# Bf16 term splitting through PSUM, a bf16 spike product and per-head exponentials in a four-layer kernel

## The reference

```
# layers 0 and 3: projections
q = (h @ Wq) * 8 ** -0.5;  k = h @ Wk;  v = h @ Wv
# layer 2, feed-forward of the spiking block; lif_scan is a leaky integrate-and-fire scan over tokens
s1 = lif_scan(x1 @ W1.T + b1)          # 0 or 1, 512 features
s2 = lif_scan(s1 @ W2.T + b2)          # 128 features
# layer 3, latent attention
p = softmax(gq @ gk.T + causal)        # 8 heads, 64 latents per query
```

## Time and profile before

| | us |
|---|---|
| median of 3 runs (lowest to highest) | 1788.99 (1785.4 to 1790.18) |
| profiled execution, its own time | 1789.75 |
| its span, first to last instruction | 1788.0 |
| DVE busy | 1332.3 (75%) |
| PE busy | 1250.5 (70%) |
| ACT busy | 879.0 (49%) |
| POOL busy | 248.0 (14%) |

### The profile page before, as it was taken

One profiled execution on the slowest core, in us unless ns is written; L12 is line 12 of the kernel. 1 busy time (PEld: TensorE's weight loads), 2 busy tenths in 40 slices (PEclk: granted clock), 3 DMA queues, 4 the chain that ended last, 5 costly groups with the idle time before them and its releaser, 6 DMA issues. The chain is left out here.

```text
span 1788.0 us, 29542 instructions
## 1 busy us (share of the span) xinstructions
PE 1250.5 (70%) x10539; PEld 612.1 (34%) x10540; DVE 1332.3 (75%) x3509; ACT 879.0 (49%) x1678; POOL 248.0 (14%) x274
## 2 busy tenths in 40 slices
PE   4799999999999997566973543040314789833776
PEld 2122222222222224346962431020113456622445
DVE  5899999999999953365448236959697779667773
ACT  4079999999999996221211113040002446612453
POOL 4000000000000000013310333030003231100223
PEclk9589999999999999667995676575655797965668
DMA  1101100001000000000004431000001402021000
GB/s 56 49 2 28 28 21 20 20 26 30 22 20 20 20 2 16 1 28 1 1 1 181 112 77 33 0 1 1 0 0 38 140 11 52 21 103 56 21 22 30
DMA packets 43229, 58.57 MB, mean 33 GB/s; under 512 B 11993, under 2 KB 33564, under 8 KB 42684
## 3 DMA queue, kind: packets, MB, share of 16 engines
q1 hardware_dynamic: 37851, 49.95, 9.4%
q0 software_dynamic: 3968, 6.01, 1.3%
q10 hardware_dynamic: 1264, 0.72, 0.2%
HBM read 29.81 MB, written 13.63 MB: 24 GB/s over the span
## 5 line engine op out<-in xcount | busy, mean ns | idle before, releaser
L724 ACT ACTIVATE l0att_probs<-l0att_ps_sv 128x512 f32<-128x512 f32 x1024 | 555.9, 595 | 84.4 <-PE l0att_ps_sv L694 72.6
L761 DVE TENSOR_REDUCE l0att_half_negmax<-l0att_ps_m 128x1 f32<-128x1024 f32 x480 | 547.2, 1215 | 6.3 <-PE l0att_ps_m L633 6.3
L663 PE MATMUL l0att_ps_sv<-l0att_probs,l_V_aug 128*32 128x256 f32 x4096 | 331.2, 392 | 5.3 <-ACT l0att_pv_sb L715 5.3
L694 PE MATMUL l0att_ps_sv<-l_Q,l_K 51*128 51x512 bf16 x1024 | 201.0, 389 | 2.5 <-ACT l0att_probs L724 0.2
L633 PE MATMUL l0att_ps_m<-l_K,l_Q 48*128 48x512 bf16 x960 | 186.1, 385 | 11.1 <-DVE l0att_half_negmax L761 7.1
L663 PEld LDWEIGHTS l0att_ps_sv<-l0att_probs,l_V_aug 128*32 128x32 f32 x4096 | 83.3, 108 | 199.1 <-issue 104.7
L694 PEld LDWEIGHTS l0att_ps_sv<-l_Q,l_K 51*128 51x128 bf16 x1024 | 49.6, 93 | 216.7 <-ACT l0att_probs L724 204.1
L350 PE MATMUL ada_ps<-ident_sb,xn 128*128 128x128 f32 x112 | 31.3, 442 | 87.5 <-DVE xn L338 87.0
L413 POOL CAST l0att_nm<-l0att_negmax 128x16 bf16<-128x16 f32 x16 | 3.2, 198 | 514.1 <-DVE l0att_negmax L737 514.1
L2554 ACT ACTIVATE l3loc_probs<-l3loc_ps_s 128x320 f32<-128x320 f32 x128 | 48.9, 435 | 36.1 <-PE l3loc_ps_s L2533 35.5
L2030 PE MATMUL l2spk_ps<-l_X,l_spikes_l_w2T 128*128 128x512 f32 x32 | 16.5, 680 | 68.3 <-DVE l_X L2054 68.3
(11 more groups left out here) (598 smaller groups left out, 2355.9 us busy)
## 6 DMA issues: line engine op xcount, KB each, us to landing
l_Q<-l_qp SPq DMA_DIRECT2D x188, 32.0 KB
l_K<-l_kp SPq DMA_DIRECT2D x188, 32.0 KB
l1ffn_W<-in_l_expert_w_dram SPq DMA_DIRECT2D x1, 4096.0 KB
l3f_experts_l_w<-in_l_w_dram SPq DMA_DIRECT2D x2, 2048.0 KB
l_sorted_in<-l1ffn_zeros SPq DMA_DIRECT2D x1, 3072.0 KB
l1exp_rows<-l_sorted_in SPq DMA_DIRECT2D x6, 512.0 KB, 8.5
l_sorted_out<-l1exp_y SPq DMA_DIRECT2D x6, 512.0 KB
l_Q<-l_q_parts SPq DMA_DIRECT2D x18, 128.0 KB
```

The costliest lines, as they stand in the source:

```text
L663: mm = pe.matmul(ps_v[32 * c:32 * c + 32, cols], V_aug[:, kt, h, :], probs[:, kt % 2, c, cols], start=(kt == 0 and part == 0), stop=(kt == ...
L694: pe.matmul(ps_s[:, (n + i) % 3, :], K[at, h % HEAD_BUFS, c1(kt)], Q[at, h % HEAD_BUFS, c4(2 * pair + i)], start=True, stop=True).then_inc ...
L724: act.activation(probs[:, kt % 2, c, :], ps_s[:, n % 3, :], ACT.Exp).then_inc(expd, 1)
L761: dve.tensor_reduce(half_negmax[:, h % 2, t, half:half + 1], src, AX_X, ALU.max, negate=True).then_inc(m_read, 1)
```

## The change

Projections: after ScalarE has copied a chunk as its first bf16 term, TensorE subtracts that term in the same PSUM bank, by a bf16 matmul with the negative identity; VectorE copies the remainder as the second term, TensorE subtracts that too, and VectorE (even chunks) or ScalarE (odd) copies the third. k comes ahead of q. The factor of q is put into its weights. The float32 copy of q is made in layer 3 alone, which uses it. VectorE's and GpSimd's splitting is gone, and each term is stored when its four chunks are there.

Spikes: the first spikes are written as bf16; the weights are split into three bf16 terms during the scan; each chunk is multiplied by three terms. Every chunk's sum is released by itself and ScalarE and VectorE copy two each.

Latent: for four of the eight heads ScalarE takes the exponential straight from PSUM, with the maximum as bias, and sums it in the same instruction; the other four go as before.

Masks: DMAs of GpSimd's queue place them with all heads in buffers 0 and 1, in place of DMAs of SyncE and copies by VectorE; ScalarE copies buffer 0 to buffer 2 as before.

The core of the diff (new semaphores and changed signatures left out):

```diff
@@ stage_project_parts @@
+def stage_project_parts(nc, loads, w_name, g, name, V_aug, qp, kp, q=None, drams=(), stored=None, beside=None):
+    CHUNKS = 2 * NC4
...
+        def term(n, i):
+            return (kp, qp)[n // NC4][i][:, c4(n % NC4)]
+                for m, (parts, dram) in enumerate(zip((kp, qp), drams)):
+                    read = NC4 * (m + 1)
+                    sp.wait_ge(high_read, read)
+                    sp.dma_start(dram[0], parts[0][:]).then_inc(stored, 16)
+                    sp.wait_ge(middle_read, read)
+                    sp.dma_start(dram[1], parts[1][:]).then_inc(stored, 16)
+                    for done in low_read:
+                        sp.wait_ge(done, read // 2)
+                    sp.dma_start(dram[2], parts[2][:]).then_inc(stored, 16)
+                for s in range(CHUNKS + 4):
+                    if s < CHUNKS:
+                        if s == NC4:
+                            pe.wait_ge(scaled, 1)
+                        pe.matmul(ps[:, s, :], w[:, 1 - s // NC4, :], g.hT[:, c4(s % NC4)], start=True, stop=True,
+                                  skip_group_check=True).then_inc(full_done, 1)
+                    if 2 <= s < CHUNKS + 2:
+                        n = s - 2
+                        pe.wait_ge(high_read, n + 1)
+                        pe.matmul(ps[:, n, :], minus[:], term(n, 0), start=False, stop=True,
+                                  skip_group_check=True).then_inc(rest_done, 1)
+                    if s >= 4:
+                        n = s - 4
+                        pe.wait_ge(middle_read, n + 1)
+                        pe.matmul(ps[:, n, :], minus[:], term(n, 1), start=False, stop=True,
+                                  skip_group_check=True).then_inc(last_done, 1)
+                    if s >= CHUNKS:
+                        j = s - CHUNKS
+                        pe.wait_ge(low_read[j % 2], j // 2 + 1)
+                        for t in range(4 * j, 4 * j + 4):
+                            mm = pe.matmul(ps[:, j, c1(t % 4)], g.hT[:, c1(t)], w[:, 2, :], start=True, stop=True)
+                act.wait_ge(loads.done, loads.all)
+                act.activation(w[:, 0, :], w[:, 0, :], ACT.Identity, scale=L0_K ** -0.5).then_inc(scaled, 1)
+                for s in range(CHUNKS + 4):
+                    if s < CHUNKS:
+                        act.wait_ge(full_done, s + 1)
+                        if q is not None and s >= NC4:
+                            act.activation(q[:, c4(s - NC4)], ps[:, s, :], ACT.Identity)
+                        act.activation(term(s, 0), ps[:, s, :], ACT.Identity).then_inc(high_read, 1)
+                    n = s - 4
+                    if n >= 0 and n % 2 == 1:
+                        act.wait_ge(last_done, n + 1)
+                        act.activation(term(n, 2), ps[:, n, :], ACT.Identity).then_inc(low_read[1], 1)
+                    j = s - CHUNKS
+                    if j >= 0:
+                        act.wait_ge(v_done, j + 1)
+                        act.activation(V_aug[:, 4 * j:4 * j + 4, :, 0:L0_K],
+                                       ps[:, j, :].rearrange("p (t h k) -> p t h k", t=4, h=L0_H), ACT.Identity)
+                for s in range(CHUNKS + 2):
+                    if s < CHUNKS:
+                        dve.wait_ge(rest_done, s + 1)
+                        dve.tensor_copy(term(s, 1), ps[:, s, :]).then_inc(middle_read, 1)
+                    n = s - 2
+                    if n >= 0 and n % 2 == 0:
+                        dve.wait_ge(last_done, n + 1)
+                        dve.tensor_copy(term(n, 2), ps[:, n, :]).then_inc(low_read[0], 1)
+                if beside is not None:
+                    beside(pool)
@@ stage_l2_spikes @@
+        w2_terms = st.sb("w2_terms", [P, 3, 4, P], BF16)
+        hidden = X[:, 0:2, :].rearrange("p g s -> p (g s)").bitcast(BF16).rearrange("p (g s) -> p g s", g=4)
+                pe.matmul(ps_t[:, 0, :], g.ident[:], w2[:].rearrange("p f e -> p (f e)"), start=True, stop=True,
+                          skip_group_check=True).then_inc(term_left, 1)
+                for i in range(2):
+                    pe.wait_ge(term_read, i + 1)
+                    pe.matmul(ps_t[:, 0, :], minus[:], w2_terms[:, i].rearrange("p f e -> p (f e)"), start=False,
+                              stop=True, skip_group_check=True).then_inc(term_left, 1)
+                pe.wait_ge(term_read, 3)
-                        mm = pe.matmul(ps[:, j, :], w2[:, f, :], X[:, f, c4(j)], start=(f == 0), stop=(f == 3))
-                mm.then_inc(h2_done, 1)
+                        for i in range(3):
+                            mm = pe.matmul(ps[:, j, :], w2_terms[:, i, f, :], hidden[:, f, c4(j)],
+                                           start=(f == 0 and i == 0), stop=(f == 3 and i == 2), skip_group_check=True)
+                        if f == 3:
+                            mm.then_inc(h2_done, 1)
+                for i in range(3):
+                    act.wait_ge(term_left, i + 1)
+                    act.activation(w2_terms[:, i].rearrange("p f e -> p (f e)"), ps_t[:, 0, :],
+                                   ACT.Identity).then_inc(term_read, 1)
-                act.wait_ge(h2_done, 1)
-                for j in range(NC4):
+                for j in range(0, NC4, 2):
+                    act.wait_ge(h2_done, j + 1)
...
+                    dve.tensor_scalar(by_chunk(hidden[:, f, :], HIDDEN_LENGTH),
-                dve.wait_ge(h2_copied, NC4)
+                dve.wait_ge(bias_ready, 1)
+                for j in range(1, NC4, 2):
+                    dve.wait_ge(h2_done, j + 1)
+                    dve.tensor_scalar(tokens_of(in_steps, OUT_LENGTH, 0, j), by_chunk(ps[:, j, :], OUT_LENGTH), 0.5,
+                                      half_b[:], ALU.mult, ALU.add).then_inc(h2_by_vector, 1)
+                dve.wait_ge(h2_copied, NC4 // 2)
+                dve.wait_ge(h2_by_vector, NC4 // 2)
@@ layer2_spiking @@
+        for_spikes = Loads(nc, d, st, "spikes", "l2_w2T", "l2_b2", "minus16")
...
+def load_mask_rows(eng, d, Q, K, buf, placed):
...
+        eng.dma_start(operand[buf][0:MASK_ROWS],
+                      bcast(d[name].unsqueeze(1), MASK_ROWS, GROUP, S + WINDOW)).then_inc(placed, 16)
@@ stage_l3_latent @@
+    SUMMED = 4
-                        pe.wait_ge(sub_ready, t - 3)
+                        pe.wait_ge(expd, t - 3)
-                        act.activation(probs[:, t % PROBS], sc[:, t % 2], ACT.Exp).then_inc(expd, 1)
+                        if t >= 2:
+                            act.wait_ge(rden_ready, t - 1)
+                        for h in range(SUMMED):
+                            act.activation(probs[:, t % PROBS, h, :],
+                                           ps_a[:, t % 4, h * LATENTS:(h + 1) * LATENTS], ACT.Exp,
+                                           bias=neg_top[:, t % 2, h:h + 1], accum_out=den[:, t % 2, h:h + 1])
+                        act.activation(probs[:, t % PROBS, SUMMED:], sc[:, t % 2], ACT.Exp).then_inc(expd, 1)
...
-                        link(dve.tensor_reduce(top[:, b, :], s3, AX_X, ALU.max))
...
+                        dve.tensor_reduce(neg_top[:, b, :], s3, AX_X, ALU.max, negate=True).then_inc(top_ready, 1)
+                        dve.wait_ge(top_ready, t + 1)
+                        dve.tensor_tensor(sc[:, b], s3[:, SUMMED:, :],
+                                          bcast(neg_top[:, b, SUMMED:].unsqueeze(2), P, LAT_H - SUMMED, LATENTS),
+                                          ALU.add).then_inc(sub_ready, 1)
-                        link(dve.tensor_reduce(den[:, b, :], probs[:, pb], AX_X, ALU.add))
+                        link(dve.tensor_reduce(den[:, b, SUMMED:], probs[:, pb, SUMMED:], AX_X, ALU.add))
@@ stage_l3_local @@
-                            pe.wait_ge(mask_copied[grp % GROUP_BUFS], 2)
+                            if grp % GROUP_BUFS < 2:
+                                pe.wait_ge(mask_placed[grp % GROUP_BUFS], 16 * 2)
+                            else:
+                                pe.wait_ge(mask_copied, 2)
+                act.wait_ge(mask_placed[0], 16 * 2)
...
+                    act.activation(operand[2][0:MASK_ROWS], operand[0][0:MASK_ROWS], ACT.Identity)\
+                       .then_inc(mask_copied, 1)
@@ layer3_attention @@
+        for_parts = Loads(nc, d, st, "parts", "l3_wqkv", "minus16")
...
-        load_mask_rows(nc.sync, d, Q, K, mask_placed)
+        mask_placed = [st.sem(f"mask_placed{b}") for b in range(2)]
...
+            def load_masks(pool):
+                for b in range(2):
+                    load_mask_rows(pool, d, Q, K, b, mask_placed[b])
+            stage_project_parts(nc, for_parts, "l3_wqkv", g, "l3proj", V_aug, qp, kp, q, (k_parts, q_parts), stored,
+                                load_masks)
@@ lay_out @@
-        "ident16": bits16(np.eye(P)),
+        "ident16": bits16(np.eye(P)), "minus16": bits16(-np.eye(P)),
```

(51 more changed lines are left out.)

66 lines of the change are left out of this document (14 added, 52 removed).

## The result

The changed kernel takes 1765.88 us (median; 1763.52 to 1768.7, 4 runs) against 1789.08 us before: ratio 0.9873, 95% interval [0.9858, 0.9888]. Forecast were 1772 and a range of 1762 to 1783. The profiled execution has a span of 1766.3 us, 21.7 less than before.

A forecast was written before the change was run, and what follows sets the result against it. Stages follow one another behind barriers; VectorE's chain bounds the projections, a ring over all engines the latent loop. Terms -6.6 - 1.7 - 3.3 - 2.7 - 3.0 = -17.3 against 1789.75 gave 1772.5, so 1772; range 1762 to 1783.

The forecast's parts named there:

- Layer 2 product: Layer 2 spikes product: 48 bf16 matmuls replace 32 fp32 passes and one last copy replaces four, scan starts 6.6 us earlier.
- Layer 0 projection: Layer 0 q and k splitting leaves VectorE; TensorE becomes the bound, stage ends at 39.1 instead of 40.79, -1.7 us.
- a change from bf16 back to fp32 weights: Projections on TensorE: each switch of weights takes 0.31 instead of 0.215 us, 12 times 0.1, adding 1.2 us.
- switches free: Layer 0 projection's lower bound: the changes of weights on TensorE cost nothing, -2.9 us.
- Layer 3 projection: Layer 3: the same added 4.6 us on TensorE, next matmul at 1398.7 instead of 1402.03, -3.3 us.
- Head of the latent stage: Layer 3 latent stage's first eight passes run at the high clock after shorter idle time, 3.6 instead of 6.31 us, -2.7.
- Latent loop: Layer 3 loop: subtraction and sum fall from eight heads to four; last 11 tiles gain 0.27 us each, -3.0.
- Ring: Latent loop's round over all four engines, two tiles: falls from 6.28 to 5.74 us.
- Rival (a): ScalarE bounds the latent loop: at 0.67 us per head a tile takes 3.7 us, whole kernel 1783; chance 0.12.
- Rival (b): Layer 3 mask transfers crowd the DMA engines, local stage 5.5 us late, whole kernel 1778; chance 0.06.
- Rival (c): TensorE's clock stays low in projections, product and latent loop, together +30 us, whole kernel 1820; chance 0.05.

## Why the prediction was right, and where it was not

The direction and the mechanism of each part held; 1765.88 lies 6 us below the forecast of 1772 and inside its range. From one profiled execution to the other, 1772.5 was forecast and 1768.11 measured: 2.7 of the 4.4 us are the changed stretches, 1.6 untouched code. The rest of the 6 is that the new execution lies 2.2 above the median of its runs where the old one lay 0.76 above, which is luck. The range's lower end, 1762, is not what its own bounds give: -9, -2.9, -4.5, -2.7 and -5 make -24.1, or 1765. By its own steps:

- **Layer 2 product, -6.6: right.** It gave 6.28. Low clock at the start and 0.215 per matmul were as priced (12.99 for 13.1). The last copy was mis-sized, 1.1 in place of 0.69 for the strided order, and that is the 0.3 that is missing.
- **Layer 0 projection, -1.7: mis-sized; -4.35.** The failed term is "a change from bf16 back to fp32 weights ... 12 times 0.1 = 1.2": it measured 0. Further, the sum was built on ScalarE's end at 34.46, 0.88 behind TensorE's last matmul, where the new last copy ends only 0.64 behind it (0.24 less); the low clock cost 1.68 in place of 2.17 (0.5, chance), the gap to the next stage is 0.31 in place of 0.57, and the loads behind it landed 0.5 sooner. The lower bound that I gave ("switches free, -2.9") held that term, but not the other four.
- **Layer 3 projection, -3.3: the same term; -5.31.** The last value copy ends 16.2 us behind the first matmul, not 18.0, and the gap to the next stage is 0.35, not 0.5.
- **Head of the latent stage, -2.7: right in place (-2.69), incomplete.** I took the clock as high and stopped there; it fell 7 us later instead, and 2.04 came back. The low stretch that lay from 1414.3 on came earlier and was 3.4 us longer, and its price was left out.
- **Latent loop, -3.0: right.** Ring 5.75 against 5.74; -3.43.
- **Rival (a):** with four heads ScalarE is busy 24.95 of 35 us and bounds nothing. Its price per head, 0.47 to 0.67, was far from 0.29.
- **Rival (b):** crowding shown, cost none; the danger lay in the issuing engine, some 22 us, which the four issues on GpSimd (0.7 to 0.9 us each) avoid by their place and not by their size.
- **Rival (c):** the clock rose in each projection as before.
- **Not in the sum:** untouched stages that meet TensorE's clock at another point, -3.00 and +2.57 in this pair of traces. They happened to cancel. The changed stretches and the 2.04 given back come to -20.0 in the trace against -17.3 foretold.

## What to carry to other kernels

Splitting a float32 value into bf16 terms by TensorE, with a negative identity in the same PSUM bank, cost 0.215 us per 512 columns here, weight loads hidden, and paid because VectorE's subtractions were on the path; TensorE then became the bound of layer 0's projection. Large transfers that nobody waits for cost 22 us here because their issuing engine had to reach a barrier: put them on a queue whose engine has nothing more to issue. Before crediting an edit with 3 us, look whether the stage that shows them runs the same code: behind TensorE's idle times the clock gave or took that much between traces of equal code.

## What the runs showed of the hardware

- ScalarE's sum output is a separate ACTIVATION_READ_ACCUMULATOR of 208 ns that overlaps the next exponential: 0.29 us from head to head for 64 columns.
- TensorE's clock fell while the engine was busy too: at 1389.4 in the changed kernel, in the middle of 32 matmuls of 32 columns, to 0.50 for 17 us. And it fell behind a stand of 1.82 us (local stage) for 3.4 us and behind one of 1.38 us (layer 0) for 6.8 us; behind one of 1.47 us it did not.
- Equal code after equal idle time (12.2 us) met the rise of the clock early or late: 3.28 to 3.31 us or 3.67 to 3.68 us for 16 transposes, 3 us up to the end of the chunk stage.
- An engine that issues small transfers behind 4.8 MB on its queue was held 15.35 us by one issue.
- PSUM to SBUF, 512 columns: 0.60 (ScalarE) and 0.69 (VectorE) in order, 1.13 and 1.08 into a strided order of steps.
